# Two transformer blocks on one core: the first block's four attention batches written out as one interleaved program

## The chip, the cores and the metric

The kernel runs on one core of one Trainium2 chip. A core has five engines with a queue of instructions each: TensorE (PE, matrix products into PSUM), VectorE (DVE), ScalarE (ACT, functions from tables), GpSimd (POOL) and SyncE (SP, which here only issues DMAs). The metric is the device time of one execution in microseconds (us).

## The reference

Two blocks follow each other on an activation x of 4 batches x 512 tokens x 128. Each block is `x = x + s * silu(f)`, where s is an attention on the layer norm of x, and f a mixture of eight experts on the same norm. Each token goes through one expert: 128 -> 512 -> 128, in the first block with a gelu.

The first block's attention, for one batch:

```
q = rms_norm(x @ w_q + b_q) per head of 8;  k = rms_norm(x @ w_k + b_k);  v = x @ w_v + b_v   (4 heads of v for 16 of q)
attn   = q @ k.T / sqrt(8), kept for 64 tokens back, 0 elsewhere
means  = mean(sigmoid(attn)) + 0.5                 # over all 512 keys
fit    = 1 / (means * sum over tokens(1 / means))
p      = softmax(attn * fit inside the window)
out    = (p @ v) @ w_o + b_o
```

So the scores are needed twice: once for the sum of sigmoids (taken as a tanh) that gives `fit`, and once, scaled by it, for the softmax. `fit` of a batch needs all 512 tokens of its first pass. The second block's attention is another, windowed one, followed by a perceptron.

## The kernel before, in words

The kernel is written engine by engine, with semaphores by hand. Its phases are: norm, route (which expert a token goes to), attention with experts, gather, join; then the same for the second block, with a perceptron ahead of the last join. Tokens are scattered by POOL into `sorted_x`, so that each of 24 tiles of 128 tokens belongs to one expert; the results come back by 16 gathers from `sorted_y`.

Attention is a loop over the four batches (`attention_phase`, used for both blocks). At the end of each turn all engines meet: each adds to `arrived` and SP then clears the semaphores and lets them go (L76 to L92). Within a turn the order on each engine is written out:

- TensorE projects v, then q and k with the tokens as stationary operand, so that tokens lie on partitions (L671, L680). Then four expert tiles: turn the input (L699), up (L702), down (L710).
- VectorE normalises q and k and splits each into three bf16 parts whose sum is the fp32 value (L545 to L550, L488 to L493): 8 columns of a head become 48, laid against each other so that one bf16 product over 48 rows gives fp32-like scores. TensorE turns these back in 12 groups of eight (L689), and ScalarE and VectorE take turns to copy them from PSUM (L857, L484).
- First pass, eight units of 64 tokens x 8 heads x 2: mask and scores on TensorE (L741, L746), tanh on ScalarE (L868), then on VectorE the sum of the tanh (L568) and the maximum of the scores (L570). Three PSUM slots.
- Two more expert tiles, and `fit` on VectorE (L580 to L597); q is scaled, split and turned again.
- Second pass, eight units: mask and logits turned round (keys on partitions, L774, L778), exp (L893), and for each pair of units the weighing: 32 fp32 products with the probabilities stationary and 9 columns of v moving (L800), then the division, turning and output projection (L635, L638, L807, L810).

SP issues each expert tile's five loads three tiles ahead (`WS = 3`, L442 to L447) and its store (L437).

Of the kernel before, what the change touches and what calls it, by code (L numbers as in the profile page):

```python
# [24 lines left out]
WS = 3  # L25
# [33 lines left out]
def block_kernel(nc, a, out, dbg):  # L59
    with ExitStack() as ctx:  # L60
# [49 lines left out]
        neghalf = sb("neghalf", [P, 256])  # L110
        maskq = sb("maskq", [P, 4, 512], BF16)
        maskk = sb("maskk", [P, 5, 512], BF16)
# [16 lines left out]
        xT = sb("xT", [P, 64 + T + 64])  # L129
# [21 lines left out]
        shifts = sb("shifts", [P, NT, H * 4])  # L151
        shr = sb("shr", [P, NT, H * 4])
        eA = sb("eA", [P, NT, H, 4])
        eB = sb("eB", [P, NT, H, 4])
        mA = sb("mA", [P, NT * H])
        osb = sb("osb", [P, H * 36])
        cs = sb("cs", [P, H, 4])
        cs2 = sb("cs2", [P, H, 4])
# [15 lines left out]
        ys = sb("ys", [P, 2, D])  # L174
# [26 lines left out]
        for n, shape in (("L0_wqk", [P, 256]), ("L1_wqk", [P, 256]), ("L0_wv", [P, 32]), ("L1_wv", [P, 128]),  # L201
                         ("L0_wo", [P, D]), ("L1_wo", [P, D]), ("L0_gw", [P, NE]), ("L1_gw", [P, NE]),
                         ("L1_mw1", [P, DF]), ("L1_mb1", [P, FC])):
            W[n] = sb(n, shape)
        W["L1_mw2"] = sb("L1_mw2", [P, FC, D])
        ROWS = {"L0_bo": D, "L1_bo": D,
# [3 lines left out]
        WIDE = {"L0_bqk": 256, "L1_bqk": 256, "L0_bv": 32, "L1_bv": 128, "L0_rms": 16, "L1_ln1g": D, "L1_ln1b": D, "L1_ln2g": D, "L1_ln2b": D, "L1_mb2": D}  # L210
        for n, k in WIDE.items():
            W[n] = sb(n, [P, k])
        rmsw = sb("rmsw", [P, 2, HD])
        vbias = sb("vbias", [P, 4, D])
# [18 lines left out]

        def sync_load(sp):
            fetch(sp, x[:, :].rearrange("p (n d) -> p n d", d=D), x3)
            for n in ("ident", "identb", "maskq", "maskk", "tab", "iota8", "cnst"):
                t = {"ident": ident, "identb": identb, "maskq": maskq, "maskk": maskk, "tab": tab, "iota8": iota8, "cnst": cnst}[n]
                src = a[n].bitcast(BF16) if n in ("identb", "maskq", "maskk") else a[n]
                fetch(sp, t[tuple(slice(None) for _ in t.shape)], src)
            for n, t in W.items():  # L240
# [12 lines left out]
        LOADS_ALL = 16 * (8 + len(W))  # L253
# [4 lines left out]
        def pool_const(po):  # L258
            po.memset(ones[:, :], 1.0).then_inc(made, 1)
            po.memset(neghalf[:, :], -0.5).then_inc(made, 1)  # L260
            po.memset(eq[:, :, :, :], 0.0).then_inc(made, 1)
            po.memset(ek[:, :, :, :], 0.0).then_inc(made, 1)
            po.memset(moe[:, :], 0.0).then_inc(made, 1)

            po.wait_ge(made, 5)
# [5 lines left out]
        def consts(eng):  # L271
            eng.wait_ge(made, 5)
# [105 lines left out]
        def attention_phase(L):  # L378
            NG = 1 if L == 0 else 4
            NK = SPLIT + 3 * NG  # L380
            KOFF = 64 if L == 0 else 32
            NV = 32 if L == 0 else 128
# [881 lines left out]
```

## Time and profile before

| | us |
|---|---|
| median of 2 runs | 1128.41 (1124.9 and 1131.91) |
| profiled execution, its own time | 1132.89 |
| its span | 1131.0 |
| busy in the span: TensorE / VectorE / ScalarE / POOL | 652.2 / 548.6 / 301.9 / 118.2 |
| mean granted TensorE clock | 0.684 |

The span counts from the first to the last instruction of the profile. A granted clock of 1.0 is 2.4 GHz, 0.5 is 1.2 GHz. In the rows PE is a matrix product, PEld the load of its stationary operand; an fp32 product shows as two records, so x8 with 128 columns is four products. In square brackets stands how long the engine was idle before, and what ended it.

### The profile page before, as it was taken

To read this page: it belongs to the slowest core of one execution; us is meant where nothing else is said; L and a number is where in the kernel's file an instruction comes from. 1 tells how busy PE (TensorE), PEld (TensorE's weight loads), DVE (VectorE), ACT (ScalarE), POOL (GpSimd) and SP (SyncE) were. 2 spreads that over 40 slices of the span, in tenths; PEclk is the share of its full clock that TensorE was granted. 3 is DMA by queue.
4 is the path that set the end of the run, shared out by engine and by line. 5 is a ranking of instruction groups with operands and counts; after the bars stand their busy time and mean duration, and the time that the engine had idled before them with its cause. 6 is when DMAs were issued, how large, how long until landed. Compare 5 with 4: busy or idle time off the path is not lost.

```text
span 1131.0 us, 17176 instructions
## 1 busy us (share of the span) xinstructions
PE 652.2 (58%) x6564; PEld 510.8 (45%) x6608; DVE 548.6 (49%) x1386; ACT 301.9 (27%) x584; POOL 118.2 (10%) x139
## 2 busy tenths in 40 slices
PE   0542658656765786483463567556755675575155
PEld 0531436544653565262452456444634554464033
DVE  0354380656156415831547275647564576556232
ACT  0201433244224423341010123132313312232023
POOL 4223000000000000003315000000000000000500
PEclk9999966576667856685555575577558557755588
DMA  6003200320040013000000410230022003200101
GB/s 204 0 16 91 80 6 2 91 58 5 2 119 28 5 45 100 4 5 23 15 0 33 116 39 6 52 90 12 0 70 79 5 0 77 72 5 2 35 1 37
DMA packets 69458, 46.05 MB, mean 41 GB/s; under 512 B 13368, under 2 KB 60986, under 8 KB 69434
## 3 DMA queue, kind: packets, MB, share of 16 engines
q1 hardware_dynamic: 66970, 39.97, 12.8%
q0 software_dynamic: 2464, 5.77, 1.7%
q8 instruction: 14, 0.23, 0.1%
q14 instruction: 10, 0.08, 0.0%
HBM read 37.85 MB, written 7.86 MB: 40 GB/s over the span
## 4 chain that ended last, share of the span: by engine, by line
DMA 33%; PE 25%; DVE 17%; issue 12%; ACT 6%; SPq 4%; POOL 3%; DVEq 0%; POOLq 0%; ACTq 0%
DMA sorted_y<-ys 29%; PE ps_score L702 7%; PE ps_score L710 4%; DVE gm L570 3%; DVE tsum L568 3%; DVE gm L574 3%; DMA b2r<-in_L_b2e 3%; DVE v L515 2%; PE ps_turn L689 2%; ACT hT L839 2%; SPq L198 2%; PE ps_proj L680 2%; PE ps_score L962 2%; PE ps_proj L671 2%; ACT kT L857 1%
## 5 line engine op out<-in xcount | busy, mean ns | idle before, releaser
L702 PE MATMUL ps_score<-xgT,w 128*128 128x128 f32 x384 | 89.8, 407 | 39.2 <-ACT xgT L836 39.2
L800 PE MATMUL ps_turn<-v,pT 128*64 128x9 f32 (+1 forms) x2048 | 103.2, 266 | 11.8 <-ACT pT L893 11.1
L800 PEld LDWEIGHTS ps_turn<-v,pT 128*64 128x64 f32 x2048 | 99.6, 204 | 16.1 <-ACT pT L893 13.4
L456 POOL TENSOR_TENSOR ys<-ys,b2r 128x128 f32<-128x128 f32 x48 | 26.0, 543 | 739.4 <-ACT ys L847 739.2
L702 PEld LDWEIGHTS ps_score<-xgT,w 128*128 128x128 f32 x384 | 76.7, 297 | 54.7 <-ACT xgT L836 54.7
L839 ACT ACTIVATE hT<-ps_score,b1s 128x128 f32<-128x128 f32 x192 | 54.7, 368 | 88.9 <-PE ps_score L702 88.9
L699 PE MATMUL ps_score<-ident,xg 128*128 128x128 f32 x48 | 19.7, 411 | 92.3 <-DMA b2r<-in_L_b2e 60.6
L484 DVE COPY kT<-ps_turn 128x1024 bf16<-128x1024 bf16 x16 | 11.1, 692 | 126.9 <-PE ps_turn L689 126.9
L710 PE MATMUL ps_score<-w,hT 128*128 128x128 f32 x384 | 72.4, 363 | 0.0
L710 PEld LDWEIGHTS ps_score<-w,hT 128*128 128x128 f32 x384 | 71.5, 283 | 0.0
L893 ACT ACTIVATE pT<-ps_score 128x1024 f32<-128x1024 f32 x64 | 62.7, 1024 | 28.7 <-PE ps_score L778 28.0
L836 ACT ACTIVATE xgT<-ps_score 128x128 f32<-128x128 f32 x48 | 13.5, 281 | 192.3 <-PE ps_score L699 192.3
L689 PE MATMUL ps_turn<-identb,eq 128*128 128x128 bf16 x512 | 39.2, 238 | 30.4 <-DVE eq L493 14.5
L699 PEld LDWEIGHTS ps_score<-ident,xg 128*128 128x128 f32 x48 | 9.4, 197 | 100.2 <-DMA b2r<-in_L_b2e 64.5
L340 PE MATMUL ps_turn<-ident,xs 128*128 128x128 f32 x32 | 8.7, 434 | 77.8 <-DVE xs L306 77.8
L671 PE MATMUL ps_proj<-L_wv,xT 128*128 128x32 f32 (+1 forms) x128 | 29.6, 417 | 36.1 <-DVE xT L500 22.2
L689 PEld LDWEIGHTS ps_turn<-identb,eq 128*128 128x128 bf16 x512 | 33.4, 107 | 36.0 <-DVE eq L493 16.0
L635 DVE RECIPROCAL wtot<-ps_turn 128x16 f32<-128x16 f32 x16 | 4.1, 258 | 93.7 <-PE ps_turn L800 93.7
L741 PE MATMUL ps_score<-maskq,identb 128*128 128x512 bf16 x60 | 26.9, 511 | 35.4 <-DVE gm L570 21.4
L671 PEld LDWEIGHTS ps_proj<-L_wv,xT 128*128 128x128 f32 x128 | 27.9, 330 | 38.4 <-DVE xT L500 24.2
L680 PE MATMUL ps_proj<-L_wqk,xT 128*128 128x256 f32 x64 | 30.9, 645 | 23.9 <-DVE v L515 23.7
L568 DVE TENSOR_REDUCE tsum<-pT 128x8 f32<-128x1024 f32 x32 | 38.7, 1210 | 9.4 <-ACT pT L868 9.4
(212 smaller groups left out, 1245.5 us busy)
## 6 DMA issues: line engine op xcount, KB each, us to landing
w<-in_L_w1e SPq DMA_DIRECT2D x48, 256.0 KB, 2.8
w<-in_L_w2e SPq DMA_DIRECT2D x48, 256.0 KB, 3.0
xg<-sorted_x SPq DMA_DIRECT2D x48, 64.0 KB, 1.9
b2r<-in_L_b2e SPq DMA_DIRECT2D x48, 64.0 KB, 3.2
sorted_y<-ys SPq DMA_DIRECT2D x48, 64.0 KB, 1.6
sorted_x<-moe POOLq DMA_DIRECT2D x2, 768.0 KB, 7.2
out<-x SPq DMA_DIRECT2D x4, 256.0 KB, 2.3
b1s<-in_L_b1e SPq DMA_DIRECT2D x48, 2.0 KB, 2.7
```

The costliest lines, as they stand in the source:

```text
L568: st(nc.vector.tensor_reduce(tsum[:, t, 8 * hf:8 * hf + 8], th[:, n % 2, :].rearrange("p (h k) -> p h k", k=128), AX.X, ALU.add))
L570: nc.vector.tensor_reduce(gm[:, t, 8 * hf:8 * hf + 8], src.rearrange("p (h k) -> p h k", k=128), AX.X, ALU.max).then_inc(s_mx, 1)
L574: nc.vector.tensor_reduce(gm[:, t, 32 * hf:32 * hf + 32], src.rearrange("p (h k) -> p h k", k=32), AX.X, ALU.max).then_inc(s_mx, 1)
L671: ins = te.matmul(o, xT[:, p0:p0 + P], W[f"L{L}_wv"][:, :], start=True, stop=True)
L680: te.matmul(o, xT[:, 64 + t * P:64 + (t + 1) * P], W[f"L{L}_wqk"][:, :], start=True, stop=True).then_inc(s_qkp, 1)
L689: ins = te.transpose(dst[:, pr * P:(pr + 1) * P], src[:, t, 2 * pr:2 * pr + 2, :].rearrange("p h r -> p (h r)"), identb[:, :])
L699: te.transpose(ps_score[:, k, 512:640], xg[:, j % WS, :], ident[:, :]).then_inc(s_ex, 1)
L702: ins = te.matmul(ps_score[:, k, c * P:(c + 1) * P], w1[:, j % WS, c * P:(c + 1) * P], xgT[:, k, :], start=True, stop=True)
L710: ins = te.matmul(ps_score[:, k, 512:640], hT[:, k, c * P:(c + 1) * P], w2[:, j % WS, c * D:(c + 1) * D], start=(c == 0), stop=(c == FC - 1))
L800: ins = te.matmul(o, w_, r, start=True, stop=True)
L839: ins = nc.scalar.activation(hT[:, k, c * P:(c + 1) * P], ps_score[:, k, c * P:(c + 1) * P], ACT.Gelu if L == 0 else ACT.Relu, bias=b1s[:, ...
L893: nc.scalar.activation(pT[:, u % 4, :], ps_score[:, u % 2, :], ACT.Exp).then_inc(s_p, 1)
```

## The change

Only the first block's attention is rewritten; `attention_phase` keeps the second block. The four turns with meetings become one straight program, `attention0`, in which every engine walks the same 6 x 11 steps (b from -1 to 4, k from 0 to 10). In step (b, k) it does, where they exist: unit k - 3 of the second pass of batch b - 1, unit k of the first pass of batch b, a piece of the preparation of batch b + 1, a piece of the fitness of batch b, and by the table `GROUP_AT` a group of two expert tiles.

- q and k are projected with the weights stationary, so that they come out turned (a head's 8 values on partitions). The squares are summed and the inverse roots spread by fp32 products with 0/1 matrices (`sel`, `rsel`, `fsel`).
- The three bf16 parts are put in their rows by DMAs from SP: 12 for q, 12 for k, 18 for the scaled q (`pack`), each 64 KB but six small ones. The 12 groups of turnings and their copies are gone.
- The masks of both passes are 64-row products; the PSUM slots are two, shared by both passes.
- In the weighing v is stationary, 32 columns wide, and 256 columns of probabilities move: four fp32 products a unit into four strips of 32 partitions. Its result is copied, turned back, divided and projected.
- The expert bias is added by VectorE, and gelu is one activation of 1024 columns for two tiles.
- At the start SP waits for the zero fill and loads eight more constants; `WS` is 4 in both blocks. The gather of the first block waits for the last store and the last `fit_q`.

ScalarE's order in a batch before: a function for a whole stage at a time.

```order
L831 ACT_TABLE_LOAD
L831 ACTIVATE rr<-ss 128x128 [waits 0_ms]
L836 ACTIVATE xgT<-ps_score 128x128 [waits 0_expert_xT]
L839 ACT_TABLE_LOAD
L839 ACTIVATE hT<-ps_score,b1s 128x128 [waits 0_expert_up]
```

And now in batch 1, steps 2 to 5 (L701 is tanh, L709 exp, L732 gelu, L694 the square root, L716 the copy of the weighed values).

```order
L694 ACT_TABLE_LOAD
L694 ACTIVATE shared<-shared 128x128 [waits a0_mean_square]
L729 ACTIVATE xgT<-ps_turn 128x256 [waits a0_expert_up,a0_expert_x_turned]
L732 ACT_TABLE_LOAD
L732 ACTIVATE hT<-hT 128x1024 [waits a0_expert_biased]
L709 ACT_TABLE_LOAD
L709 ACTIVATE pT<-ps_score 128x1024 [waits a0_logits]
L701 ACTIVATE pT<-ps_score 128x1024 [waits a0_tanh_summed,a0_scores]
L738 ACTIVATE ys<-ps_turn 128x256 [waits a0_expert_stored,a0_expert_down]
```

What moved: a table load now stands ahead of each gelu, and another ahead of the exp behind it.

TensorE in batch 1, steps 5 and 6 (L581 and L591 are mask and logits, L540 and L552 mask and scores, L604 the weighing, L625 and L631 a group's turning and up, L640 its down, L611 the turning back).

```order
L591 MATMUL ps_score<-xlT,kT 128x64 x16
L540 MATMUL ps_score<-maskq,eyeb 128x512 [waits a0_max]
L552 MATMUL ps_score<-ek,eq 64x128 x16
L604 MATMUL ps_proj<-pT,v 32x4x64 [waits a0_probs]
L625 MATMUL ps_turn<-ident,xg 128x128 [waits a0_expert_biased,a0_expert_in0]
L631 MATMUL ps_turn<-xgT,w 128x128 [waits a0_expert_y,a0_expert_x_kept]
L581 MATMUL ps_score<-eye,maskt 128x512 [waits a0_probs]
```

And somewhat later, when the group's gelu is done:

```order
L640 MATMUL ps_turn<-w,hT 128x128 [waits a0_expert_biased,a0_expert_hidden]
L611 MATMUL ps_proj<-ident,osb 128x128 [waits a0_context_kept]
L604 MATMUL ps_proj<-pT,v 32x4x64 [waits a0_head,a0_probs]
```

Before, the units of the first pass stood behind each other with nothing between, and waited for the slots alone:

```order
L741 MATMUL ps_turn<-maskq,identb 128x512 [waits 0_max]
L746 MATMUL ps_turn<-kT,qT 64x128 x16
L699 MATMUL ps_score<-ident,xg 128x128 [waits 0_expert_copied,0_expert_in1,0_max]
```

What moved: experts, weighing and both passes are now in one line on TensorE, with waits for ScalarE and VectorE between them.

The diff, cut to its core:

```diff
-WS = 3
+WS = 4
...
+            sp.wait_ge(filled, 32)
+            for kp in kpk:
+                for par in range(2):
+                    fetch(sp, kp[64 * par + SPLIT:64 * par + SPLIT + 3, :, :], a["ones3"].bitcast(BF16))
+            fetch(sp, rsel, a["rsel"])
+            fetch(sp, fsel, a["fsel"])
...
-            po.memset(eq[:, :, :, :], 0.0).then_inc(made, 1)
-            po.memset(ek[:, :, :, :], 0.0).then_inc(made, 1)
...
+        def attention0():
...
+            GROUP_AT = {(-1, 4): 0, (0, 2): 1, (0, 4): 2, (0, 6): 3, (0, 8): 4, (1, 2): 5, (1, 5): 6, (1, 8): 7,
+                        (2, 2): 8, (2, 5): 9, (2, 8): 10, (3, 2): 11}
...
+                def square_sums(b):
+                    te.wait_ge(s_qe, b + 1)
+                    te.wait_ge(s_ke, b + 1)
+                    misc.take(te, s_mean, b + 1)
+                    for z, src in enumerate((sqq, sqk)):
+                        for t in range(NT):
+                            ins = te.matmul(M[32 * t:32 * t + 32, 0:P], sel[:, z, :], src[:, t * P:(t + 1) * P],
+                                            start=z == 0, stop=z == 1, skip_group_check=True)
...
+                def weigh(b, u):
+                    n = NU * b + u
+                    te.wait_ge(s_p, n + 1)
+                    if u == 0:
+                        te.wait_ge(s_v, b + 1)
+                    if u % 2 == 0 and n > 0:
+                        te.wait_ge(s_hd, n // 2)
+                    for g in range(4):
+                        hf, par = g % 2, g // 2
+                        o = CT[32 * g:32 * g + 32, :].rearrange("p (j b q) -> p j b q", j=4, b=2)[:, :, u % 2, :]
+                        ins = te.matmul(o, v0[b % 2][:, u, 32 * g:32 * g + 32],
+                                        pT[:, n % 2, par * 512 + hf * 256:par * 512 + hf * 256 + 256], start=True, stop=True)
+                    ins.then_inc(s_pv, 1)
...
+                for b in range(-1, B + 1):
+                    for k in range(11):
+                        if b >= 1 and k >= 3:
+                            logits(b - 1, k - 3)
+                        if 0 <= b < B and k < 8:
+                            scores(b, k)
+                        if (b, k - 1) in GROUP_AT:
+                            experts_down(GROUP_AT[b, k - 1])
+                        if b + 1 < B:
+                            if k < 2:
+                                project_in(b + 1, k)
+                            if k == 2:
+                                square_sums(b + 1)
+                            if k in (3, 4):
+                                spread_rms(b + 1, k - 3)
+                        if 0 <= b < B:
+                            if k == 2:
+                                values(b)
+                            if k == 8:
+                                inverse_sum(b)
+                            if k == 9:
+                                turn_fitness(b)
+                            if k == 10:
+                                spread_fitness(b)
+                        if b >= 1 and k >= 4:
+                            u = k - 3
+                            if u in (3, 5, 7):
+                                turn_back(b - 1, u // 2 - 1)
+                            weigh(b - 1, u - 1)
+                            if u in (4, 6):
+                                project_out(b - 1, u // 2 - 2)
+                        if (b, k) in GROUP_AT:
+                            experts_up(GROUP_AT[b, k])
...
+                def pack(dst, parts, terms, done, n, loaded):
+                    for s in range(3):
+                        sp.wait_ge(done, n + s + 1)
+                        for m, part in enumerate(terms):
+                            if part == s:
+                                for par in range(2):
+                                    r = 64 * par + HD * m
+                                    sp.dma_start(dst[r:r + HD, :, :], parts[64 * par:64 * par + 64, s, :]).then_inc(loaded, 16)
...
+            def gather(po):
+                if stored is not None:
+                    po.wait_ge(*stored)
+                    po.wait_ge(*spread_done)
```

## Rows read from the trace of the kernel before

**Rows 1.** Stages: us; busy us of PE, PEld, DVE, ACT, POOL; clock; DMA
```profile
75.10:523.50 448.40, 287.09 (x3124) 217.27 (x3152) 207.77 (x396) 152.64 (x280) 29.98 (x41) 0.71 0.15 41
201.00:308.80 107.80, 72.38 (x781) 55.05 (x788) 51.91 (x98) 38.07 (x70) 2.76 (x6) 0.66 0.15 40
246.00:260.00 14.00, 6.49 (x87) 2.35 (x80) 13.79 (x13) 5.37 (x6) 0.00 (x0) 0.50 0.00 0
523.50:547.00 23.50, 0.00 (x0) 0.00 (x0) 5.54 (x9) 2.58 (x5) 14.83 (x16) 0.50 0.17 45
```
**Rows 2.** Timeline, first pass of batch 1: start, duration, engine, line, operation
```profile
241.98 0.44 PE L746 MATMUL ps_score<-kT,qT 48*64 48x128 bf16 x16
...
247.57 1.03 PE L741 MATMUL ps_score<-maskq,identb 128*128 128x512 bf16 x2 [1.18 <-DVE gm L570]
247.61 1.02 ACT L868 ACTIVATE pT<-ps_score 128x1024 f32<-128x1024 f32 x1 [1.36 <-DVE gm L570]
248.54 0.66 PE L746 MATMUL ps_score<-kT,qT 48*64 48x128 bf16 x16
248.68 1.23 DVE L570 TENSOR_REDUCE gm<-ps_turn 128x8 f32<-128x1024 f32 x1
```
**Rows 3.** Timeline, an expert's up: batch 1 of either block
```profile
228.93 2.08 PE L702 MATMUL ps_score<-xgT,w 128*128 128x128 f32 x8 [0.37 <-ACT xgT L836]
...
742.87 1.16 PE L702 MATMUL ps_score<-xgT,w 128*128 128x128 f32 x8 [1.29 <-ACT xgT L836]
```
**Rows 4.** Timeline of the start, and the fill's line among the DMA issues
```profile
1.11 3.51 POOL L261 MEMSET eq<- 128x4096 bf16 x1
...
21.51 0.43 SPq L198 DMA_DIRECT2D L_mb<-in_L_mb  x1
26.92 1.65 DVE L297 BATCH_NORM_STATS2 stats<-x 128x6 f32 x8 [26.92 <-DMA L_mb<-in_L_mb]
...
sorted_x<-moe POOLq DMA_DIRECT2D x2, 768.0 KB, 7.2
```
**Rows 5.** Timeline of the first expert's loads, and b2r among the DMA issues
```profile
98.57 0.36 SPq L442 DMA_DIRECT2D xg<-sorted_x  x1
...
101.97 0.33 SPq L442 DMA_DIRECT2D xg<-sorted_x  x1
...
103.75 0.47 PE L699 MATMUL ps_score<-ident,xg 128*128 128x128 f32 x1 [19.51 <-DMA b2r<-in_L_b2e]
...
b2r<-in_L_b2e SPq DMA_DIRECT2D x48, 64.0 KB, 3.2
```
**Rows 6.** Groups by form: line, shapes, count, busy us, mean ns, idle before
```profile
L540 DVE TENSOR_TENSOR k<-k,rr 128x512 f32<-128x512 f32 x4 | 2.8, 691 | 0.1
```
**Rows 7.** Chain of waits: the perceptron's up; timeline: old weighing, two clocks
```profile
1070.69 5.89 PE ps_score L962 x8
1077.83 3.70 PE ps_score L962 x8
...
498.49 2.04 PE L800 MATMUL ps_turn<-v,pT 128*64 128x9 f32 x64
505.25 3.59 PE L800 MATMUL ps_turn<-v,pT 128*64 128x9 f32 x64
```
**Rows 8.** Timeline, from the gather to the next norm
```profile
524.43 0.96 POOL L1061 DMA_INDIRECT moe<-sorted_y,pos  x1 [0.30 <-issue]
...
547.00 1.65 DVE L297 BATCH_NORM_STATS2 stats<-x 128x6 f32 x8 [0.44 <-DVE x L1083]
```
**Rows 9.** Waits of TensorE in the second block (total, times, longest); chain's scatter
```profile
PE ps_score L699 <- DMA b2r<-in_L_b2e: 26.9, 6, 8.7
...
591.78 32.87 issue
```
**Rows 10.** Timeline of ScalarE at a change of table
```profile
490.60 1.28 ACT L893 ACT_TABLE_LOAD   x1
...
491.89 4.00 ACT L893 ACTIVATE pT<-ps_score 128x1024 f32<-128x1024 f32 x4
```

More of the change, by code:

```diff
@@ L912, in mlp_phase @@
             hxT = xlT[:, 0:2 * T].rearrange("p (h n) -> p h n", h=2)
-            hidden = [b.rearrange("p a (b n) -> p (a b) n", n=T) for b in (th, pT[:, 0:2, :])]
+            hidden = [b[:, :, :].rearrange("p a (b n) -> p (a b) n", n=T) for b in (th, pT)]
             def vec(dv):
@@ L984, in route_phase @@
         def route_phase(L):
+            counted = [ps_score[:, 0, 512 * n:512 * n + 512] if L == 0 else ps_proj[:, n, :] for n in range(2)]
             s_pick = sem(f"{L}_picked")
@@ L1156, in _ @@
             route0_pe(te)
-            attn0.pe(te)
+            attn0_pe(te)
             norm1.pe(te)
@@ L1197, in shape_constants @@
                            penal(pair(sided, 0), 4), penal(pair(sided, 3), 4)], 1)
-    c["maskk"] = np.stack([penal(causal(0).T, 8), penal(causal(1).T, 8), penal(causal(2).T, 8),
-                           penal(sided(0).T, 8), penal(sided(NU - 1).T, 8)], 1)
+    c["maskk"] = np.stack([penal(sided(0).T, 8), penal(sided(NU - 1).T, 8)], 1)
+    c["maskt"] = np.stack([penal(np.tile(causal(u), (2, 1)), 1) for u in range(3)], 1)
+    p = np.arange(P)
+    c["eye64"] = bf16_bits(p[:, None] % 64 == np.arange(512) % 64)
+    c["eyeb"] = bf16_bits(p[:, None] % 64 == p % 64)
+    owner = p // 64 * 8 + p % 8
+    c["ones3"] = bf16_bits(np.ones((3, 8, T)))
+    c["sel"] = np.stack([np.arange(32) == 16 * z + owner[:, None] for z in range(2)], 1).astype(np.float32)
+    c["fsel"] = np.stack([(np.arange(64)[:, None] // 4 == owner) & (np.arange(64)[:, None] % 4 == t) for t in range(NT)], 1).astype(np.float32)
+    row = np.stack([np.arange(P) // 32, np.arange(P) // 16 % 2, np.arange(P) % 16], 1)
+    c["rsel"] = np.stack([np.stack([(row[:, 0:1] == t) & (row[:, 1:2] == z) & (row[:, 2:3] == owner) for t in range(NT)], 1)
+                          for z in range(2)], 1).astype(np.float32)
     tab = np.zeros((P, 64), np.float32)
@@ L1225, in laid_out @@
     stored = [8 * hf + 4 * par + j for hf in range(2) for j in range(4) for par in range(2)]
-    cols = np.array([h * HD + e for h in stored for e in range(HD)])
+    stored = np.array([h * HD + e for h in stored for e in range(HD)])
+    spread = np.array([(8 * par + pr) * HD + e for par in range(2) for e in range(HD) for pr in range(8)])
     a = {}
```

805 lines of the change are left out of this document (607 added, 198 removed).

## The prediction

> **What bounds the kernel now.** I read the busy times by stage first, then the timeline of one batch of the first layer, and last the waits and the list of DMA issues. The stages [rows 1]: 448.4 us for the four batches of the first layer's attention and experts, 107.8 of them for the second batch, then 23.5 us for gather and join. In a steady batch of 107.8 us TensorE is busy 72.4, VectorE 51.9, ScalarE 38.1: none is full, so a batch is a chain of stages that take turns. TensorE's granted clock is 0.66 there (0.71 over the four), which is 2.4 GHz a third of the time and 1.2 GHz the rest [rows 1]. The reader should see three stretches in the timeline. In the first pass each unit costs VectorE two reductions of 1.23 us, 2.4 with their overlap, and it is busy 13.79 of 14.0 us; TensorE and ScalarE wait for it [rows 1, 2]. Around the experts VectorE and ScalarE are idle and TensorE alternates with ScalarE [rows 3]. In the second pass TensorE and ScalarE alternate and VectorE waits. The change puts these stretches of two batches side by side.
>
> **The change, step by step.** The sums go against the profiled execution (span 1131.0, own time 1132.9); the median of the runs is 1128.4, 4.5 lower.
>
> *Start: +10.5 us.* VectorE begins when the last of the loads has landed, 26.9 [rows 4]. The queue of SP now stops after twelve fixed loads until the zero fill has landed. The two removed memsets of 3.5 us (one row stands for both) let POOL issue the fill some 7 us sooner, ending near 5.2; with 7.2 us to landing [rows 4] that is 12.4. Then 8 new loads at 0.5 to 1 us of issue (4 to 7 us), the other weights, 26 of them before as now, at 0.43 to 1.1 us of issue each (some 15 us, the last of them at 21.5), and the 5.4 us from the start of the last to VectorE: 37 to 40 for 26.9. I take 37.4.
>
> *Up to the first unit.* Expert 0's weights were there at 103.75 [rows 5], as the scatter sets it. TensorE's order now has group 0 (two tiles) ahead of the first scores; its second tile is issued 3.4 us later [rows 5], so with the 10.5 it is ready at 118. Up (3.3), copy, bias, gelu and down then stand in a row: 10 us. First scores at 128. The packing of q and k (24 DMAs at some 0.5 us of issue) is done by then, behind the scatter.
>
> *Prices of a step.* Two reductions stay 2.4 us. An activation of 1024 is 1.02 [rows 2]. An elementwise pass over 512 is 0.69 [rows 6]; normalise with its split is three of those and two shorter casts, 3.0, and there are three such per batch. Four fp32 matmuls of 128 columns take 2.08 us at 1.2 GHz and 1.16 at 2.4 [rows 3]; for a group's eight, 2.3 to 4.2, I take the middle, 3.3, its down 3.0. The turns, sums and values, fp32 too, go by the same rows. The mask and scores of a unit are 1.03 + 0.66 at 1.2 GHz now [rows 2]; with the mask in the 64-row form of its neighbours, two halves at once, I take 0.9, and 0.8 for the logits. The new weighing is four fp32 matmuls of 256 columns a unit. Fp32 with 512 columns takes 5.89 / 4 = 1.47 us mostly at 1.2 GHz and 3.70 / 4 = 0.92 at 2.4 [rows 7], so one after another they are 1.85 us at 2.4 GHz and 3.4 at 1.2 GHz (twice the cycles); if all four column strips ran together, 0.5. The old one took 2.04 or 3.59 per pair of units [rows 7], so the new one is no cheaper in itself: 1.0 to 6.8 per pair. I take 2.0 a unit, nearest to the serial rows. The Trainium skill, TensorEngine Tiling, Tiling Modes and Performance Considerations, says that swapping the stationary operand with a 32-wide one gives four tiles that execute in parallel. By that, the sum would be about 38 us lower (rival B has this); no row of this trace shows column strips together, only row halves: 16 score matmuls of 128 columns in 0.44 us [rows 2], half of what 16 x 53 ns would be.
>
> *A full batch (1 and 2).* Steps 0 and 1: VectorE's 2.6 each, 5.2. Step 2: reduce 2.4, mean, square root 0.3, values 3.0 and their copy 0.5, then the expert group: turn and copy 0.9, up 3.3, bias 0.8, gelu 1.1: 12.3. Step 3: a table load 1.3, exp and tanh 2.0, then VectorE alone: 2.4 + 2.1 (inverse root) + 1.4 (spread) + 3.0 = 12.2. Steps 4 and 5: scores, weighing, group up, bias, gelu, table load, exp, tanh in one chain on TensorE and ScalarE: 16.3. Step 6, where TensorE's weighing stands behind VectorE's reduction and head: 8.0. Steps 7 to 10 and the batch's tail: five weighings 10, group up and down 6.3, turning back 3.3, four output projections with ScalarE's turn 4, logits 2.4, bias, gelu and copies 2.9, fitness 1.4, VectorE's fit_q and heads ahead of them in its order 6.1: 36.4. Sum 90.4, against 107.8 before.
>
> *The others.* Batch 0 has no second pass but four groups: 65.5 (steps 7.0, 13.1, 9.9, 9.0, 2.4, 6.0, 3.5, 6.7, 7.9). Batch 3 has one group and no next batch to prepare: 62. The last second pass, alone: 8 x (logits 0.8 + weighing 2.0) + turning and projecting 13, with the tail 38. Loop: 65.5 + 180.8 + 62 + 38 = 346, so it ends at 474 for 521.
>
> *Gather and join: part of the gain.* 16 gathers, one each 1.26 us (0.96 + 0.30), stood bare between attention and join [rows 8]. POOL may now start at the last fit_q, 38 us before the end, and needs 20: hidden, unless the second pass shrank below that. The join is left with 7 to 8 us. The second layer's norm starts at 481.5 for 547.0: 65.5 us gained.
>
> *Second layer: 16 us.* With four weight buffers the fourth tile's weights no longer wait for tile 0's result. The layer's waits for the last of a tile's loads are 26.9 us in six; the longest, 8.7, is the first tile behind the scatter, and the other 18.2 are nearly all fourth tiles [rows 9]. I take 16. The new memsets lie under the scatter (32.9 us of it [rows 9]) and cost nothing; were that cover gone, 1 us.
>
> *Table loads.* They rise from 3 per batch to about 5: exp and gelu alternate. A load is 1.28 us and the next activation starts at once [rows 10]. Of some 20 about 8 are bare, after a gelu with exp's logits ready, 10 us, in the steps above; the rest run while ScalarE waits. The Trainium skill, ScalarE: Activation LUTs, section Table sets, speaks against this change: batch by set, since each switch is about 2.7 us. By that figure the bare ones would be 11 us more; the trace disagrees, its 1.28 has no drain behind it.
>
> Sum: 1132.9 - 65.5 - 16 = 1051.4, less 4.5 for the median: **1047 us**.
>
> **Rivals.** *A, the forecast*, 1047; alone 1022 to 1078. *B, column strips together, and TensorE warm.* Weighing 0.5 for 2.0: 32 x 1.5, of which 0.8 lie on the path, 38, so 1009 by the strips alone; groups at 2.3 for 3.3, 20 stretches: 20 more, about 990. For it: the clock rises within the perceptron's first 6 us of unbroken fp32 matmuls and stays there [rows 7], and the new loop gives TensorE longer unbroken stretches. Against: the clock stays at 0.5 through 246 to 260 with TensorE busy 6.49 of 14.0 us [rows 1]. *C, TensorE cold and strips serial.* Weighing 3.4 for 2.0 adds 36, groups 18, values and sums 12: 1113. For it: in-order TensorE with waits for both other engines in each step. *D, slower: the packing.* 42 DMAs a batch from 64 partitions into 8, each issued by SP, whose queue also carries the experts' weights. The nearest row lands 64 KB in 3.2 us [rows 5]. If landings pipelined they would cost SP 20 us of 90 and stay hidden. If those into the same 8 partitions landed one after another, 42 x 3.2 = 134 us a batch replaces 90.4, and four batches give 1047 + 4 x 43.6 = 1221. It decides slower from (22.6 + 81) / 4 = 26 us a batch, so 116 / 42 = 2.8 us per transfer. Against it: the first tile's five loads, issued from 98.57 on, are there together at 103.75 [rows 5].
>
> **Chances.** A 0.48, B 0.22, C 0.22, D 0.08. 2% is 22.6 us, about what a measurement of this kernel can tell. A and B are faster; C is around the edge (1106), a third of it faster: faster 0.78, same 0.14, slower 0.08. The range leaves out D and the outer ends of B and C: 988 to 1118.
>
> **What would show it.** VectorE's first statistics near 37. First scores near 128 with the scatter's end before them. Batches about 90 apart. The weighing's four matmuls near 0.5 or near 2 to 3.4 us a unit tells B from A and C; the granted clock in the loop (I expect 0.75) tells C from A. Gathers that end before the last head; a join of 8 us. In the second layer no wait of TensorE for the fourth tile. Wrong would be: units waiting for packed q or k (D), a group waiting for its weights because SP stands at a packing's wait, or a batch still above 105 with all engines below 60%, an ordering that only moved the waits.

## The result, and the profile after

The changed kernel takes 1049.56 us (median of 1047.18 and 1051.93) for 1128.41; the ratio is 0.9301, 95% interval 0.9148 to 0.9455. The profiled execution took 1051.93 us with a span of 1050.1. The forecast was 1047 for the median and 1051.4 for a profiled execution, so the sum is met within 3 us. Its terms are not, and most of what follows is about them.

First the busy times by stage of the changed kernel, cut at the first scores of the four batches, the last batch's first logits and the last output. Columns: stretch; its length; busy us of PE, PEld, DVE, ACT, POOL; granted clock; DMA share, GB/s.

```profile
131.90:207.80 75.90, 46.41 (x362) 36.62 (x360) 35.89 (x52) 20.70 (x28) 3.67 (x5) 0.73 0.39 98
207.80:295.10 87.30, 59.37 (x581) 41.01 (x581) 43.37 (x74) 36.15 (x45) 2.21 (x3) 0.70 0.49 96
295.10:380.60 85.50, 59.51 (x581) 41.65 (x580) 40.82 (x68) 35.94 (x45) 2.17 (x3) 0.72 0.34 70
380.60:448.00 67.40, 44.51 (x476) 26.34 (x474) 29.85 (x49) 23.55 (x29) 13.15 (x15) 0.58 0.20 31
448.00:478.70 30.70, 20.49 (x252) 9.88 (x252) 3.36 (x12) 12.02 (x17) 2.72 (x3) 0.72 0.04 10
```

A steady batch takes 87.3 or 85.5 us for 107.8, with TensorE busy 59.4 for 72.4 and the clock at 0.70 to 0.72 for 0.66 [rows 1]. TensorE is busy 68% of it, as before (67%): a batch is still a chain of stages, only fewer of them stand alone. The five stretches are 346.8 us, where the forecast had 346.

The timeline of the start: SP's queue behind the zero fill, the last constant, and VectorE's first statistics [rows 4].

```profile
13.68 1.75 SPq L213 DMA_DIRECT2D kT<-in_ones  x2
...
29.20 0.43 SPq L213 DMA_DIRECT2D L_mb<-in_L_mb  x1
35.05 1.64 DVE L317 BATCH_NORM_STATS2 stats<-x 128x6 f32 x8 [35.05 <-DMA L_mb<-in_L_mb]
```

The start is 8.1 us later (35.05 for 26.92), where the forecast had 10.5.

Timeline of the weighing (L604), once at 2.4 and once at 1.2 GHz (granted clock 1.00 and 0.50 in these rows); x8 is one unit's four fp32 products of 256 columns [rows 7].

```profile
246.72 0.64 PE L604 MATMUL ps_proj<-pT,v 128*32 128x256 f32 x8
...
263.94 1.08 PE L604 MATMUL ps_proj<-pT,v 128*32 128x256 f32 x8
```

A unit takes 0.64 or 1.08 us, where the prediction had taken 2.0 from rows with one product behind another.

Timeline of TensorE and of SP's queue in batch 0: the input turning of groups 3 and 4, the first logits of batch 0, and SP's packing DMAs (q of the next batch, then the scaled q).

```profile
180.65 0.69 PE L625 MATMUL ps_turn<-ident,xg 128*128 128x128 f32 x2 [5.19 <-DMA b2r<-in_L_b2e]
195.71 0.69 PE L625 MATMUL ps_turn<-ident,xg 128*128 128x128 f32 x2 [3.47 <-DMA b2r<-in_L_b2e]
231.81 0.61 PE L581 MATMUL ps_score<-eye,maskt 64*128 64x512 bf16 x2 [5.26 <-DMA xlT<-xn]
...
161.21 8.97 SPq L954 DMA_DIRECT2D eq<-xs  x12
...
218.60 8.62 SPq L954 DMA_DIRECT2D xlT<-xn  x12
```

Twelve packings take SP's queue 8.6 to 9.0 us, 0.72 to 0.75 us each; the experts' loads stand behind them in the same queue, and TensorE, in order, stops for both: 8.7 us for two groups' weights and 5.3 for the packed q, 4.6 of these behind the last packing's issue (227.22 to 231.81).

The table load of exp behind a gelu [rows 10], and the start of the second layer's norm with the second layer's waits for weights [rows 8, 9]:

```profile
254.69 1.28 ACT L709 ACT_TABLE_LOAD   x1
255.99 1.02 ACT L709 ACTIVATE pT<-ps_score 128x1024 f32<-128x1024 f32 x1
...
485.61 1.65 DVE L317 BATCH_NORM_STATS2 stats<-x 128x6 f32 x8 [0.43 <-DVE x L1615]
```

```profile
PE ps_score L1245 <- DMA b2r<-in_L_b2e: 8.5, 2, 7.7
```

The norm starts at 485.6 for 547.0, and from there to the end it takes 564.5 us for 584.0.

Last, the gathers beside the last second pass, and the chain from the turned values (L611) to VectorE's reciprocal (L859):

```profile
431.61 0.99 POOL L1593 DMA_INDIRECT moe<-sorted_y,pos  x1 [32.69 <-issue]
437.10 1.06 PE L611 MATMUL ps_proj<-ident,osb 128*128 128x128 f32 x4
441.46 0.26 DVE L859 RECIPROCAL wtot<-ps_proj 128x16 f32<-128x16 f32 x1 [3.58 <-remote]
...
450.39 0.94 POOL L1593 DMA_INDIRECT moe<-sorted_y,pos  x1 [0.30 <-issue]
```

The turning ends at 438.16 and VectorE starts 3.3 us later, with nothing else to do. This delay was in no part of the forecast.

### The profile page after: what moved, and what is told of

Its sections match the earlier page's. It is cut to its first block, busy times and chain, and to the rows that moved or that the text cites. A ratio compares the mean times of both kernels' runs of the same rounds, so it can differ in the third digit from the quotient of the medians.

```text
span 1050.1 us, 15348 instructions
## 1 busy us (share of the span) xinstructions
PE 610.5 (58%) x5772; PEld 455.3 (43%) x5772; DVE 506.2 (48%) x1270; ACT 282.8 (27%) x476; POOL 106.3 (10%) x125
## 4 chain that ended last, share of the span: by engine, by line
PE 28%; DMA 21%; DVE 19%; issue 13%; ACT 7%; SPq 7%; POOL 3%; another core or an unknown queue 1%; DVEq 0%; POOLq 0%; ACTq 0%
DMA sorted_y<-ys 18%; DVE gm L1151 3%; PE ps_score L1248 3%; DVE v L1115 2%; SPq L954 2%; PE ps_turn L631 2%; PE ps_proj L604 2%; PE ps_score L1490 2%; DVE gm L806 2%; DVE tsum L809 2%; PE ps_proj L366 1%; POOL sorted_x L1581 1%; PE ps_proj L369 1%; ACT pT L701 1%; PE ps_proj L1496 1%
## 5 line engine op out<-in xcount | busy, mean ns | idle before, releaser
L806 DVE TENSOR_REDUCE gm<-ps_score 128x8 f32<-128x1024 f32 x32 | 39.1, 1222 | 63.5 <-ACT pT L701 63.2
L1339 PE MATMUL ps_turn<-v,pT 128*64 128x36 f32 x1024 | 57.1, 299 | 6.2 <-ACT pT L1421 5.5
L1339 PEld LDWEIGHTS ps_turn<-v,pT 128*64 128x64 f32 x1024 | 55.0, 222 | 8.6 <-ACT pT L1421 6.7
L709 ACT ACTIVATE pT<-ps_score 128x1024 f32<-128x1024 f32 x32 | 32.7, 1024 | 65.9 <-PE ps_score L591 50.6
L1248 PE MATMUL ps_score<-xgT,w 128*128 128x128 f32 x192 | 40.1, 374 | 14.7 <-ACT xgT L1371 14.7
L640 PE MATMUL ps_turn<-w,hT 128*128 128x128 f32 x192 | 35.9, 363 | 18.1 <-ACT hT L732 17.9
L631 PE MATMUL ps_turn<-xgT,w 128*128 128x128 f32 x192 | 40.1, 394 | 7.0 <-ACT xgT L729 7.0
L1248 PEld LDWEIGHTS ps_score<-xgT,w 128*128 128x128 f32 x192 | 34.2, 268 | 22.5 <-ACT xgT L1371 22.5
L640 PEld LDWEIGHTS ps_turn<-w,hT 128*128 128x128 f32 x192 | 33.3, 270 | 20.3 <-ACT hT L732 20.1
L631 PEld LDWEIGHTS ps_turn<-xgT,w 128*128 128x128 f32 x192 | 37.0, 296 | 11.3 <-ACT xgT L729 11.3
L604 PE MATMUL ps_proj<-pT,v 128*32 128x256 f32 x256 | 28.4, 541 | 21.7 <-DVE head L862 21.0
L701 ACT ACTIVATE pT<-ps_score 128x1024 f32<-128x1024 f32 x32 | 32.7, 1021 | 20.0 <-PE ps_score L552 18.7
L1115 DVE SCALAR_TENSOR_TENSOR v<-ps_proj,tab,moe 128x128 f32<-128x128 f32 x128 | 33.4, 342 | 8.7 <-PE ps_proj L1217 6.5
```

Of the source, the lines that this page charges most:

```text
L604: ins = te.matmul(o, v0[b % 2][:, u, 32 * g:32 * g + 32], pT[:, n % 2, par * 512 + hf * 256:par * 512 + hf * 256 + 256], start=True, stop= ...
L631: ins = te.matmul(bank[:, c * P:(c + 1) * P], w1[:, 2 * (g % 2) + n, c * P:(c + 1) * P], xgT[:, n, :], start=True, stop=True)
L640: ins = te.matmul(EX[:, n * P:(n + 1) * P], hT[:, n, c * P:(c + 1) * P], w2[:, 2 * (g % 2) + n, c * D:(c + 1) * D], start=(c == 0), stop=( ...
L701: nc.scalar.activation(th[:, n % 2, :], SLOT[PLACE["p1", b, n] % 2], ACT.Tanh, scale=0.5).then_inc(s_th, 1)
L709: nc.scalar.activation(pT[:, n % 2, :], SLOT[slot], ACT.Exp).then_inc(s_p, 1)
L806: nc.vector.tensor_reduce(gmx[b % 2][:, t, :].rearrange("p (a r) -> p a r", a=2)[:, :, 4 * hf:4 * hf + 4], SLOT[PLACE["p1", b, n] % 2].rea ...
```

## The experiments

Each kernel is the changed kernel with the edit shown. Every run comes with a ratio to the kernel before on the same chip; one hundredth is 11.3 us. A difference of two ratios and one of two medians can be some us apart; where it matters both are given. The base is the changed kernel run again.

**The base.**

> The changed kernel unchanged, as the base of this group. By every theory its first result within 0.5%: a ratio to the kernel before near 0.93.

Measured: 1045.42 us, ratio 0.9172 (0.9116 to 0.9229). That lies in the first result's wide interval, and is the value that the others are held against. Its loop, from first scores to last output, took 344.6 us.

**Do the column strips run together?**

```diff
+                    for g in range(4):
+                        ...
+                        o = CT[32 * g:32 * g + 32, :]...          # strips_own;  strips_one: CT[0:32, :]
+                        te.matmul(o, v0[b % 2][:, u, 32 * g:32 * g + 32], pT[...], start=True, stop=True)
                     for g in range(4):
```

> Changed kernel, with the four weighing products of each unit issued twice, each time into their own four strips of 32 partitions (the first set is overwritten by the second). Theory 1, the strips run together: a unit is 0.53 us at 2.4 GHz and 1.08 at 1.2 GHz in the changed kernel, so a doubled unit is 1.07 or 2.0, TensorE works 28 us more, and with the path share of 0.8 that the prediction used the time is about 1065 to 1078. Theory 2, the strips run one after another and a product is simply cheap: the same doubling. This run is the measure for the next one.

> As the run before, but the four extra products all go into the first strip (overwritten by the right ones behind them). Theory 1, strips run together only because they are different: the extra four take 4 x 0.46 = 1.85 us at 2.4 GHz and 3.4 at 1.2 GHz (by the fp32 products of 512 columns of the perceptron), a unit is 2.4 to 4.5 us instead of 1.07 to 2.0, and the time is 40 to 80 us above the run with the strips of their own. Theory 2, strips don't matter: the same time as that run, within 5 us.

Measured: 0.9319 (0.9261 to 0.9377) with the strips of their own, 0.9566 (0.9505 to 0.9627) with one strip: 1059.1 and 1082.7 us. The timeline of one unit, at a granted clock of 0.50 in the first run and 0.58 in the second; L604 are the extra products and L609 the right ones. Strips of their own:

```profile
255.72 1.08 PE L604 MATMUL ps_proj<-pT,v 128*32 128x256 f32 x8 [3.73 <-DVE head L867]
256.54 1.11 PE L609 MATMUL ps_proj<-pT,v 128*32 128x256 f32 x8
```

One strip for the four extra products:

```profile
421.73 3.10 PE L604 MATMUL ps_proj<-pT,v 128*32 128x256 f32 x7 [3.78 <-DVE head L867]
424.20 0.65 PE L609 MATMUL ps_proj<-pT,v 128*32 128x256 f32 x3
424.62 0.63 PE L604 MATMUL ps_proj<-pT,v 128*32 128x256 f32 x1
424.63 1.10 PE L609 MATMUL ps_proj<-pT,v 128*32 128x256 f32 x5
```

The same eight products take 1.9 us (255.72 to 257.65) where each strip gets two, and 4.0 us (421.73 to 425.73) where the first strip gets five, although the clock is a little higher there. So products in different strips run together, and products in the same strip do not: theory 1. The Trainium skill, TensorEngine Tiling, Tiling Modes and Performance Considerations, says that four tiles of 32 columns can execute matrix products in parallel; here the runs agree with it, and the neighbouring rows from which I had priced the weighing did not bear on it. The expected 40 to 80 us between the two was a miss: 23.6 us by the medians, 28 by the ratios. TensorE is busy 58 us longer (112.5 for 54.1 in these two lines), so four to five tenths of it lie on the path, not the 0.8 that I had used. The first of the two runs was also below its expected 1065 to 1078.

**What do the table loads cost?**

```diff
-                    nc.scalar.activation(h_, h_, ACT.Gelu).then_inc(s_hid, 1)
+                    nc.scalar.activation(h_, h_, ACT.Tanh).then_inc(s_hid, 1)
```

> Changed kernel with the expert's gelu replaced by tanh, whose table holds exp too, so that the first block's loop reloads no table between gelu and exp (the experts' result is another function). My theory: of the 20 loads in the loop only the 6 that stand directly ahead of a ready exp are bare, 1.28 us each, so 8 us less: about 1041. Rival, by the Trainium skill's page ScalarE: Activation LUTs, section Table sets, about 2.7 us for each switch: some 14 switches vanish, 38 us, about 1012. Rival 2: a wait elsewhere takes the place, no change, 1049.

This kernel leaves out the gelu, so its result is another one. Measured: 0.9181 (0.9125 to 0.9237), 1040.4 us; against the base no difference can be told by the ratios. The profiles of the two say a little more: from the first scores of batch 1 to those of batch 3 (two full batches with five of the six bare loads) 165.8 us for 170.4 in the base and 172.8 in the first profile. Groups of table loads on ScalarE in the loop with tanh:

```profile
L694 ACT ACT_TABLE_LOAD x4 | 5.1, 1283 | 0.1
L732 ACT ACT_TABLE_LOAD x4 | 5.1, 1283 | 0.1
```

Twelve loads of 20 are gone, the seven of exp and five of gelu's nine, and what vanished is 5 to 7 us: the bare ones at 1.28 us each. The 38 us that 2.7 us a switch would give are excluded.

**Is it the interleaving?**

```diff
-                for b in range(-1, B + 1):
-                    for k in range(11):
+                for b, k, f, s in STEPS:        # f: first pass and all that goes with it, s: second pass
+                    ...                         # (b, 0..10, f), then (b + 1, 3..10, s), for every b
```

> Changed kernel with the same instructions, but the second pass of a batch stands behind its own first pass (eight steps of its own) rather than beside the next batch's first pass. My theory, the gain of the loop is the interleaving: a batch then costs its first pass as batch 0 shows it (76, about 70 with three groups, 50 for the last) and then its second pass with the wait for the packed q as the last one shows it (10 + 30): 4 x 40 + 76 + 70 + 70 + 50 = 426 for the loop's 347, so about 1128, the time of the kernel before. Rival: the cheaper projections, weighing and the missing meetings carry the gain and the interleaving little: 1049 to 1075.

Measured: 0.9813 (0.9761 to 0.9866), 1112.0 us, 67 us by the medians and 72 by the ratios over the base. Busy times of its four batches:

```profile
131.40:250.00 118.60, 63.46 (x602) 46.52 (x601) 41.41 (x66) 31.62 (x42) 3.61 (x5) 0.67 0.35 82
255.50:360.00 104.50, 55.10 (x568) 38.69 (x567) 40.05 (x65) 29.84 (x38) 2.17 (x3) 0.69 0.36 65
364.00:461.00 97.00, 54.16 (x569) 37.23 (x568) 40.17 (x65) 29.96 (x38) 2.17 (x3) 0.74 0.30 57
464.40:543.00 78.60, 35.42 (x474) 21.86 (x473) 29.89 (x49) 24.50 (x30) 15.92 (x17) 0.71 0.15 27
```

The loop takes 411 us for 346.8 and the second layer's norm starts at 549.7, where the kernel before had it at 547.0. So the new operations in the old order bring nothing to the first block, and its 61 us need the new order. My 1128 was 16 us too high.

But this does not say that the cheaper operations are worth nothing. In this order the logits of a batch follow straight on its own scaled q, and TensorE waits for each packing. The groups of TensorE's logits, first in this run and then in the base, with what ended the idle time before them:

```profile
L586 PE MATMUL ps_score<-eye,maskt 64*128 64x512 bf16 x64 | 15.8, 491 | 81.6 <-DMA xlT<-xn 81.6
L581 PE MATMUL ps_score<-eye,maskt 64*128 64x512 bf16 x64 | 17.0, 509 | 9.0 <-DMA xlT<-xn 6.7 <-issue 2.0 <-ACT pT L709 0.3
```

The four waits for a packed q are 16.7 to 22.9 us each, 81.6 in all for 6.7, so 75 us more in a loop that got 67 longer (411 for the base's 344.6). Each wait holds VectorE's last steps on q, SP's 18 issues and their landing. What the order hides is thus, in size, mostly the packing that the change itself brought in. The kernel before turned its q by TensorE and had no such wait. How the old operations would do in the new order, no run shows.

**Is SP's queue the limit of the packing?**

```diff
-    sp.dma_start(dst[r:r + HD, :, :], parts[64 * par:64 * par + 64, s, :])
+    for h in range(2):
+        sp.dma_start(dst[r + 4 * h:r + 4 * h + 4, :, :], parts[64 * par + 32 * h:64 * par + 32 * h + 32, s, :])
```

> Changed kernel with each packing DMA of 64 KB split into two of 32 KB (78 DMAs a batch for 42, the same bytes). My theory: what a packing costs is its issue on SP's queue, 0.72 us each whatever its size; 36 more a batch are 26 us of SP's time, 12 of them (8.6 us) ahead of each batch's first logits, and the expert loads behind them come later: 30 to 60 us more, 1080 to 1110. Rival 1, the issue takes time by what it moves: halves cost half, no change, 1045 to 1055. Rival 2 (the prediction's D), landings into the same 8 partitions one after another: the same bytes, no change either, but then the wait from the last issue to the first logits is long.

Measured: 0.9613 (0.9551 to 0.9676), 1089.5 us, 44 us by the medians and 50 by the ratios over the base. SP's queue at the packing of the first scaled q:

```profile
245.06 16.17 SPq L955 DMA_DIRECT2D xlT<-xn  x24
```

24 halves take 16.17 us, 0.67 each, where a whole one took 0.66 to 0.75. Of the two sizes tried, a packing costs its issue, whatever it moves. The last half is issued by 261.23 and the logits start at 263.45, so no line of landings waits there. TensorE's waits in the loop grew from 6.7 to 21.8 us for the packed q and from 9.4 to 24.0 for the experts' loads, which stand behind the packings in the queue, and the first scores came 13 us later (144.8 for 131.5), behind the 48 packings of the first batch. The prediction's D had the right resource and the wrong mechanism: landings do not queue, issues do.

**Half of the packing on another queue.**

```diff
+                for b in range(-1, B + 1):           # in POOL's program
+                    for k in range(11):
+                        if b >= 0 and b + 1 < B and k in (3, 4):
+                            pack_in(po, b + 1, k - 3, (1,))
+                        if 0 <= b < B and k == 10:
+                            pack_fit(po, b, (1,))
```

> Changed kernel with half of the packing DMAs (the lower 64 partitions) issued by POOL from its own queue from the second batch on, and half of those of every scaled q. My theory, SP's queue is what is late: the fit pack is issued in 6 to 9 us instead of 12.4, the experts' loads in batch 0 no longer wait 9 us behind it and the first logits of batch 0 and 3 come 3 to 5 us sooner: 1030 to 1042. Rival: POOL's DMAs are dearer (1.26 us apiece in the gather) and they delay VectorE or land later: 1049 or more.

Measured: 0.919 (0.9132 to 0.9247), 1044.4 us: no gain over the base, and the expected 1030 to 1042 was a miss. The first logits did come sooner: those of batch 0 at 223.7 without a wait (228.3 in the base), those of batch 3 at 436.7 (442.5). But TensorE's wait for the experts' loads in batch 0 stayed (8.1 us for 9.4), and the last second pass took 37.8 us for 33.7. Its timeline, TensorE's logits (L598), the gathers and ScalarE's exp (L716):

```profile
438.23 0.42 PE L598 MATMUL ps_score<-xlT,kT 51*128 51x64 bf16 x8
438.68 0.94 POOL L1609 DMA_INDIRECT moe<-sorted_y,pos  x1 [0.30 <-issue]
439.00 0.21 PE L598 MATMUL ps_score<-xlT,kT 51*128 51x64 bf16 x1 [0.36 <-issue]
...
443.23 0.21 PE L598 MATMUL ps_score<-xlT,kT 51*128 51x64 bf16 x1 [1.20 <-issue]
...
452.42 1.94 ACT L716 ACTIVATE pT<-ps_score 128x1024 f32<-128x1024 f32 x2 [18.25 <-remote]
```

TensorE issues its products one by one with gaps of 0.4 to 1.2 us, waiting for nothing that the profile shows, and ScalarE starts 9 us behind the last of them, 2.8 us after the last gather's end (449.6).

**When the gathers run.**

```diff
-            return vec, act, pool, pe, sync, (s_yst, 16 * NG), (s_q2, B)
+            return vec, act, pool, pe, sync, (s_yst, 16 * NG), (s_sc2, NU * (B - 1) + 1)    # gather_later
+            return vec, act, pool, pe, sync, (s_yst, 16 * NG), (s_o, NT * B)                # gather_end
```

> Changed kernel with the first block's gather waiting for the last batch's first logits instead of its last scaled q. My theory: the 16 gathers (431.6 to 451.3) run while the last packing DMAs land (8.4 us from the last issue to the logits, 4.6 in batch 0) and delay them; later gathers bring the logits 4 us forward, and with 20 us they still fit in the 30 us of the last second pass: 1045 to 1047. Rival: they don't disturb each other: 1049, or a join that waits for the gather, 1052.

Measured: 0.9304 (0.9244 to 0.9364), 1054.8 us, slower than the base by 9 us (medians) to 15 (ratios): neither theory. Timeline of that pass: logits, exp, reciprocal and the last gather.

```profile
444.14 0.39 PE L581 MATMUL ps_score<-eye,maskt 64*128 64x512 bf16 x2
449.89 1.02 ACT L709 ACTIVATE pT<-ps_score 128x1024 f32<-128x1024 f32 x1 [4.25 <-remote]
452.02 0.26 DVE L859 RECIPROCAL wtot<-ps_proj 128x16 f32<-128x16 f32 x1 [17.71 <-remote]
453.77 0.61 PE L581 MATMUL ps_score<-eye,maskt 64*128 64x512 bf16 x2
460.17 0.95 POOL L1593 DMA_INDIRECT moe<-sorted_y,pos  x1 [0.30 <-issue]
464.07 1.02 ACT L709 ACTIVATE pT<-ps_score 128x1024 f32<-128x1024 f32 x1 [13.16 <-remote]
```

The logits of 444.14 are done by 444.8 and exp starts at 449.9; those of 453.77 by 454.8, and exp starts at 464.1, 3 us behind the last gather. From first logits to last output the pass takes 44.7 us.

The longest such stall lies in the run with the extra products in strips of their own. Its last gather, and ScalarE's copy of a head whose turning was done at 439.5:

```profile
452.94 0.94 POOL L1598 DMA_INDIRECT moe<-sorted_y,pos  x1 [0.30 <-issue]
...
457.52 0.28 ACT L728 ACTIVATE headT<-ps_proj 128x128 f32<-128x128 f32 x1 [26.15 <-remote]
```

That is 18 us late, and ahead of the last second pass. The run with one strip has a stall of 15 us at the same place, so the difference of those two stands within some 3 us. In all eleven profiles with the sixteen gathers beside the end of the loop, ScalarE's first activation behind them starts 2.8 to 3.8 us after the last one has ended (in one of them behind logits that were late themselves).

> Changed kernel with the first block's 16 gathers waiting for the last output projection, so that nothing of them lies beside the loop, as in the kernel before. My theory: beside the loop the gathers stall the other engines. The last second pass then takes about 24 us from its first logits to its last output (30.3 in the changed kernel, 44.7 with the gathers started 8 us later), its packed q lands 2 to 4 us sooner, and the loop ends near 467 for 478; but the 16 gathers stand bare, 20 us, so the sum is 8 to 12 us slower than the changed kernel. Rival, the stalls in that pass have another cause and the pass takes 30 us without the gathers too: 20 us slower.

Measured: 0.9209 (0.9162 to 0.9256), 1048.0 us, the same as the base within the intervals, and not the 8 to 12 us more that I had expected. The same pass without gathers:

```profile
441.03:465.46 24.43, 19.09 (x252) 9.53 (x252) 3.07 (x12) 12.05 (x17) 0.00 (x0) 0.78 0.00 1
```

24.4 us for 30.3 in the first profile, 33.7 in the base's and 44.7 above, as expected of the theory. Batch 3 to its first logits takes 64.2 us for 67.4 and 67.5. The loop ends at 465.5 and the norm starts at 490.8 for 485.6 in the first profile and 483.1 in the base's: hiding 20 us of gathers brought 5 to 8, since the rest came back as stalls.

**Four buffers in the second layer.**

```diff
-            s_ew = [sem(f"{L}_expert_in{k}") for k in range(WS)]      # WS = 4
+            s_ew = [sem(f"{L}_expert_in{k}") for k in range(3)]       # and 3 at every other use there
```

> Changed kernel with three weight buffers in the second block's loop, as before the change (the first block keeps its own four). My theory: TensorE's waits for the experts' weights return, 18 us of them (26.9 in the kernel before, 8.5 now), so 1066 to 1069. Rival: the fourth buffer gives nothing and the second block gained by something else: 1049.

Measured: 0.9371 (0.9317 to 0.9424), 1063.6 us, 18 us over the base by the medians; from the norm's start to the end 585.2 us for 564.2 in the base. TensorE's wait for the experts' last load:

```profile
PE ps_score L1246 <- DMA b2r<-in_L_b2e: 26.4, 6, 7.1
```

26.4 us in six waits for 8.5 in two (first profile): 18 of the 21 us are these.

**A shorter start, and then earlier gathers.**

```diff
+            sp.dma_start(x[:, :]..., x3).then_inc(FIRST, 16)       # then ident, L0_gw, L0_gb; the rest as before
-                loaded(dv)                                         # first norm; now ahead of the routing
+                dv.wait_ge(FIRST, 64)
-            po.wait_ge(filled, 32)                                 # now ahead of the scatter
```

> Changed kernel with two edits: half of the packing DMAs on POOL's queue (as in an earlier run, 5 to 12 us), and a start in which x, the identity and the gate's two weights are loaded first under a semaphore of their own; the first norm waits for those four alone and everything else lands beside it; POOL waits for its zero fill only ahead of the scatter. My theory: VectorE starts its statistics near 7 to 10 us instead of 35, all else follows 25 us earlier, unless the late constants hold the routing (they land near 35, the routing starts near 61 now and 36 then): 1049 - 25 - 8 = 1016. Rival: the loads compete, the routing waits for the last constant and only 10 us are gained: 1031.

Measured: 0.9034 (0.8982 to 0.9087), 1026.1 us (profiled span 1013.8). The first scores come at 108.2 for 131.5, 23 us of the 25 expected. The 8 us expected of the packing on POOL did not come, as in the run with it alone: the last second pass takes 38.1 us, with ScalarE standing until 2.9 us after the last gather. So 1026 for the expected 1016.

```diff
-                    po.wait_ge(*stored)
-                    po.wait_ge(*spread_done)
-                for t in range(NTT):
+                    po.wait_ge(*stored)
+                for t in (*range(8), *range(12, 16), *range(8, 12)):
+                    if t == 8 and stored is not None:
+                        po.wait_ge(*spread_done)
```

> Changed kernel with the short start of the run before (x, identity and gate first; all packing on SP again), and twelve of the first block's sixteen gathers issued as soon as the last expert tile is stored, beside the last batch's first pass; the other four, whose target still holds a constant, follow behind the last scaled q. By the start alone 1045 - 23 = 1022. My theory, a gather stalls whatever chain of PE, ACT and DVE it lies beside: the first pass of batch 3 gets longer by about 8 us and the last second pass shorter by as much (24 to 27 us from first logits to last output), 1017 to 1025. Rival, beside a first pass that waits for VectorE's reductions the stalls are absorbed: 1012 to 1016. Rival 2, the stall depends on SP's packing DMAs being in flight: no stall in either place, 1010.

Measured: 0.8903 (0.8863 to 0.8943), **1011.87 us**, the fastest of all. Timeline of the first statistics, the first and the last gather and the second norm, and the busy times of the last second pass:

```profile
8.58 1.65 DVE L325 BATCH_NORM_STATS2 stats<-x 128x6 f32 x8 [8.58 <-DMA L_gb<-in_L_gb]
...
377.12 0.99 POOL L1604 DMA_INDIRECT moe<-sorted_y,pos  x1 [2.13 <-DMA sorted_y<-ys]
...
409.09 0.94 POOL L1604 DMA_INDIRECT moe<-sorted_y,pos  x1 [0.30 <-issue]
...
450.08 1.65 DVE L325 BATCH_NORM_STATS2 stats<-x 128x6 f32 x8 [0.43 <-DVE x L1626]
```

```profile
419.80:443.10 23.30, 17.32 (x252) 8.85 (x252) 3.14 (x12) 11.89 (x17) 0.00 (x0) 0.87 0.00 1
```

The first pass of batch 3 with its preparation of the second, beside which twelve gathers now lie, takes 64.7 us (first scores to first logits), as in the run without gathers there (64.2), and the last pass takes 23.3. So these gathers are hidden. By the time the rival had it (1012 to 1016, no stall beside a first pass); why nothing is seen there, whether by absorption or because no stall arises, the run does not tell. Rival 2, that the packings in flight are needed, would give much the same time, but the later gathers above stalled with no packing in flight.

## Why the prediction came out right, step by step

| Term | forecast | measured | off by |
|---|---|---|---|
| start | +10.5 | +8.1 | -2.4 |
| first statistics to first scores | 90.6 | 96.8 | +6.3 |
| batch 0 | 65.5 | 75.9 | +10.4 |
| batches 1 and 2 | 90.4 each | 87.3 and 85.5 | -8.0 |
| batch 3 to its first logits | 62 | 67.4 | +5.4 |
| last second pass | 38 | 30.7 | -7.3 |
| join | 7.5 | 6.9 | -0.6 |
| second layer | -16 | -19.5 | -3.5 |

Together the terms are off by 0.3 us, taken singly by 44: that the sum came so close is luck. The mechanism of A held: the batches overlap, none of the engines is full, the second layer and the join gain what WS and the hidden gathers give. Four of its terms were mis-sized.

- **The weighing, 2.0 us a unit.** It measured 0.64 and 1.08, as rival B's strips say, and the run with one strip shows why. The 32 units take 28.4 us, 0.89 each, so this is 36 us too much (32 x 1.11). By the share of four to five tenths on the path it is an estimated 14 to 18 us of the sum, spread over the second passes of all batches. Its upper price was also off in itself: twice the cycles of 1.85 us are 3.7, not 3.4. Rival B was right in the strips and wrong in the sum. Its share of 0.8 on the path was too high, and the other half of it, a warm TensorE, did not come: the clock is 0.70 to 0.73 in the loop, and 0.58 beside batch 3's first pass. C's cold TensorE did not come either.
- **SP's queue.** I gave a packing some 0.5 us and counted its 20 us a batch as hidden; it takes 0.72, 30 a batch, and together with the experts' loads it is late in batch 0 (8.7 us) and at the first logits of batch 0 and 3 (5.3 and 4.0). The 8.7 are most of the 10.4, and the 4.0 part of the 5.4. D named the queue, and neither its 3.2 us per transfer nor its serial landings are there.
- **The first scores.** From the first statistics they took 6.3 us more than forecast. The first expert's loads are issued at 112.50, 7.9 us behind the last scatter's record (104.56), where before it was 2.5 (98.57 behind 96.03). The 24 packings of the first batch fill SP's queue until 108.78 in between. What the other 3.7 us are, no run separates.
- **The gathers "hidden, unless the second pass shrank below" 20 us.** They were beside other work and still cost it 6 to 9 us in that pass, and some 3 ahead of it. Here two errors cancel: the pass was forecast at 38 us, takes 24.4 without gathers, and the stalls gave back 6 of the 14 between. The term was measured as intended only with twelve of them moved.

The table loads were priced rightly: 20 in the loop for "some 20", six bare ones for eight, 1.28 us each. The Trainium skill's 2.7 us for a switch (ScalarE: Activation LUTs, section Table sets) is not borne out by the run with tanh. The start was near in its parts: a wait for the fill of 1.7 us, eight loads in 4.2 for 4 to 7, the weights in 11.7 for some 15.

Open is what stalls the other engines beside the gathers, and why only near and in the last second pass. One candidate, not shown, is that loads of the engines' own programs are held up behind the gathers. The traces list such transfers (kind "instruction"), but in the run with the stall of 18 us the only one near it is at 434, 23 us before ScalarE goes on, and two lie beside the twelve early gathers, where the pass is no longer (376 and 389). No run here took them away.

## What to carry to other kernels

A sum that comes out right says little about its terms: price an operation from a row of its own kind, or carry both ends of it. Here the new operations in the old order gained nothing, since their packings stood bare for 82 us, and the interleaving hid all but 7 of these. So when a run takes the order back, look at which wait grows before giving the order the credit. And work that is put beside a chain can still cost that chain: look at what it does to the starts of its neighbours, and move it to a stretch that waits for one full engine.

## What the runs showed of the hardware

- Four fp32 products with 32 stationary columns each, written to four strips of partitions, run together: 1.08 us at 1.2 GHz and 0.64 at 2.4; in one strip they add up (the extra four take 2.9 us at a granted clock of 0.58, for 0.8 at 0.50 in four strips).
- A DMA from SBUF to SBUF into a few partitions holds SP's queue for 0.66 to 0.75 us where it moves 64 KB into eight, and for 0.67 where it moves 32 KB into four.
- A table load of ScalarE takes 1.28 us, and the activation behind it starts within 0.02 us (254.69 and 255.99).
- Beside 16 indirect gathers of POOL (1.25 us apart), ScalarE and VectorE started 3 to 18 us after TensorE's result was there, and TensorE issued products singly; in eleven profiles ScalarE went on 2.8 to 3.8 us after the last gather. Beside a first pass of the same kernel, with twelve gathers, nothing of it is seen.
